# One ring of six PSUM banks for scores and maxima products in an attention stage

## The chip, the cores and the metric

One Trainium2 chip, one of its cores. The metric is the device time of the kernel in microseconds (us). Three runs of the kernel before gave 1196.69, 1202.45 and 1202.41 us, median 1202.41. The execution that was profiled took 1201.56 us, 1199.8 of them between its first and last instruction.

## The reference, cut to what matters

A transformer block in float32: layer norm, cross attention with a residual, layer norm, a mixture of experts with a residual. The change lies in the attention alone:

```
qh, kh, vh = heads of (layernorm(x) @ Wq.T), (ctx @ Wk.T), (ctx @ Wv.T + bv)   # 4 batches, 16 heads of 32
scores = einsum('bhsd,bhtd->bhst', qh, kh) / sqrt(32)        # 1024 x 1024 for each head
scores = where(t >= s, -inf, scores), but (0, 0) stays       # strictly causal
out    = softmax(scores) @ vh                                # then @ Wo.T + bo
```

## The kernel before

After the projections the attention runs in 16 loops (`NIT`), one for each batch and group of four heads (`HG`). A loop needs the queries and keys of its four heads as stacks of 96 rows (high and low parts, so that one product per block is precise enough), in one of three slots (`SLOTS`).

The work is done twice over the same stacks. First come the **maxima**: for each block of 128 queries the product with its keys, in pieces called chunks, 48 a loop (`NC`), 16 early ones for the first 512 queries (`FIRST`, with the diagonal block always at the end of the piece) and 32 late ones (`LATE`). PE writes a chunk to a PSUM bank (line 1151), DVE reduces it to a column of maxima (lines 928 and 931). When the 16 early ones are there, PE turns the columns into rows (the early turn, line 1161), ACT negates them (line 1042), and SP writes the rows by DMA into row 96 of the query stack (line 702, `place_row`). The 32 late ones are followed by a late turn in the same way. Then come the **scores**, transposed (keys on partitions), where the 97th row subtracts the maximum: 12 steps of key blocks by 512 queries, four heads each; PE writes them (line 1172), ACT takes the exponential into `p_t` (line 1064), POOL masks diagonal blocks, and PE multiplies by the values (line 1191) and by ones for the sums (line 1205).

PE's order is written out by hand. A loop has six groups of two steps. In group g, `full_width` (lines 1210 to 1224) issues eight scores of the group that follows, and between them as many chunks **of the next loop** as `SHARE[g]` says (eight numbers, one ahead of each score). Then come the values and sums of group g. The late turn of the loop stands ahead of the third score of group 0; the early turn of the next loop at the head of group `EARLY_AT`, the first group by whose start all 16 early chunks are issued:

```
PER = [sum(share) for share in SHARE]
EARLY_AT = 1 + min(g for g in range(len(GROUPS)) if sum(PER[:g + 1]) >= EARLY)
```

The first chunk of a loop (`c == 0`) is the first product of group 0. It waits for the whole load of its slot, ten DMAs (`chunk`, its wait on `loaded`). Scores cycle through banks 0 to 2 by their own number (`SB + n % SR`) and wait for the exponential three units back; chunks and turns cycle through banks 3 to 5 and wait for the maximum (or the negation) three places back. Bank 6 holds the output, bank 7 the sums. Units of narrow steps hold two or four heads in one bank (`TOGETHER`).

SP's queue is in program order too. In each loop `it` (from line 764 on):

```
place_row(2 * it + 1)                 # late row of this loop
if it > 0: store(it - 1, 1)
if it + 1 < NIT: place_row(2 * it + 2)    # early row of the next loop; waits for m_row_ready
if it + 2 < NIT:
    sp.wait_ge(step_done, it * NS + FETCH)
    load(sp, it + 2)                  # six DMAs of queries, three of keys, one of values
store(it, 0)
```

So the load of loop it + 2 is issued in loop it, for the first chunk of group 0 of loop it + 1. There are 14 such loads.

Of the kernel before, what the change touches and what calls it, by code (L numbers as in the profile page):

```python
# [9 lines left out]
ACT = mybir.ActivationFunctionType  # L10
AX = mybir.AxisListType

P = 128
B, S, D = 4, 1024, 512
H, HD = 16, 32
HG = 4
# [390 lines left out]
def project_attend_route(nc, a, m, keep):  # L407

    NIT = B * NG
    ST = S // P  # L410
    R = 3 * HD
# [4 lines left out]
    NS = len(STEPS)  # L416
    SPAN = [(max(CH * sh, P * j), CH * (sh + 1) - max(CH * sh, P * j)) for sh, j in STEPS]
    TOGETHER = [CH // w if w <= CH // 2 else 1 for _, w in SPAN]
    UNITS = [HG // n for n in TOGETHER]
    UNIT0 = [sum(UNITS[:k]) for k in range(NS + 1)]  # L420
    DIAG = [k for k, (sh, j) in enumerate(STEPS) if P * j >= CH * sh]

    FIRST = [(0, 0), (3, 1), (2, 2), (3, 2), (2, 1), (0, 2), (1, 3), (3, 0), (2, 0), (0, 1), (1, 0), (2, 3), (1, 1),
             (1, 2), (0, 3), (3, 3)]
    LATE = [(2, 5, 0), (1, 4, 1), (2, 7, 0), (0, 7, 0), (3, 5, 1), (3, 6, 1), (0, 5, 0), (3, 6, 0), (2, 7, 1),
# [3 lines left out]
    CHUNKS = [(h, i, 0, (i + 1) * P, True) for h, i in FIRST]  # L429
    EARLY = len(CHUNKS)  # L430
    for h, i, diag in LATE:
        CHUNKS.append((h, i, CH, (i + 1) * P - CH, True) if diag else (h, i, 0, CH, False))
    assert len(set(FIRST)) == HG * ST // 2 and len(set(LATE)) == HG * ST
    NC = len(CHUNKS)
    TRIED = [sum(c[3] for c in CHUNKS[:n] if c[4]) for n in range(NC + 1)]

    GROUPS = [[k, k + 1] for k in range(0, NS, 2)]
# [8 lines left out]
    INVERSIONS = {1: 1, 3: 0}  # L446
    TURN_SLOT = 2

    SHARE = [[1, 2, 0, 1, 1, 2, 1, 0], [0, 2, 0, 2, 1, 2, 1, 1], [4, 0, 1, 1, 1, 1, 0, 2], [1, 0, 0, 1, 0, 2, 2, 1],
             [1, 1, 0, 0, 1, 3, 0, 1], [2, 1, 0, 2, 1, 0, 0, 1]]  # L450

    def portions(g, chunks):
        return SHARE[g] if chunks else [0] * (2 * HG)

    PER = [sum(share) for share in SHARE]
    EARLY_AT = 1 + min(g for g in range(len(GROUPS)) if sum(PER[:g + 1]) >= EARLY)
    TAKES = [PER] * (NIT - 1) + [[0] * len(GROUPS)]
    BEFORE, total = {}, NC
# [8 lines left out]
    TURN_AT = SPOTS[EARLY + 1]  # L467
    AHEAD = [(k, h) for k in GROUPS[0] for h in range(HG)]
    RINGS = {}

    with ExitStack() as ctx:
        def sb(name, shape, dt):
# [5 lines left out]
        def sem(name):  # L478
            return ctx.enter_context(nc.semaphore(name))
# [38 lines left out]
        ks, qs, vt = [k_stack0, k_stack1, k_stack2], [q_stack0, q_stack1, q_stack2], [v_tile0, v_tile1, v_tile2]  # L518
# [28 lines left out]
        t_hi = put("t_hi", [P, KD, CH], F32R, o_at)  # L547
        t_lo = put("t_lo", [P, KD, CH], F32R, sum_at)
        bank = ctx.enter_context(nc.psum_tensor("p2_bank", [P, 8, 512], F32))
        SR, MR = 3, 3  # L550
        SB, MX, OB, DB = 0, 3, 6, 7
        VB, FB, KB = 0, 2, 4

        piece_in = [sem(f"piece_in{k}") for k in range(KD)]
# [45 lines left out]
        exp_done = sem("exp_done")  # L600
# [27 lines left out]

        ring = []
        first_ring = []  # L630

        def place(kind, n):

            RINGS[kind, n] = (MX + len(ring) % MR, ring[-MR] if len(ring) >= MR else None)
            ring.append((kind, n))

        def place_first(kind, n):

            RINGS[kind, n] = (FB + len(first_ring) % 2, first_ring[-2] if len(first_ring) >= 2 else None)
            first_ring.append((kind, n))  # L640

        for spot, n in OURS.items():
            place_first("chunk", n)
            if spot == TURN_AT:
                place_first("turn", 0)
        for it in range(NIT):
            for g in range(len(GROUPS)):
                first = sum(portions(g, TAKES[it][g])[:TURN_SLOT])
                if g == EARLY_AT and it + 1 < NIT:
                    place("turn", 2 * it + 2)  # L650
                for n in range(TAKES[it][g]):
                    if n == first and g == 0:
                        place("turn", 2 * it + 1)
                    place("chunk", BEFORE[it, g] + n)
                if TAKES[it][g] <= first and g == 0:
                    place("turn", 2 * it + 1)

        def fetch_q(eng, it, half, done):

# [24 lines left out]
        with nc.Block() as block:  # L684
# [162 lines left out]
            def _(dve):  # L847
# [62 lines left out]
                def maximum(n):  # L910
# [9 lines left out]
                    col = h * (ST // 2) + i % (ST // 2)  # L920
                    got = bank[:, RINGS["chunk", n][0], 0:w]
                    if diag:
# [104 lines left out]
            def _(act):  # L1027
# [8 lines left out]
                def negate(turn):  # L1036
# [3 lines left out]
                    if it > 0:  # L1040
                        act.wait_ge(m_placed, (turn - 1) * 16)
                    act.activation(m_row[late][:], bank[0:HG * ST // 2, RINGS["turn", turn][0], 0:P], ACT.Copy,
                                   scale=-1.0).then_inc(m_row_ready, 1)
# [9 lines left out]
                def exponential(it, k, u):  # L1053
                    w, m = SPAN[k][1], TOGETHER[k]
                    n = it * UNIT0[NS] + UNIT0[k] + u
                    act.wait_ge(scored, n + 1)
                    if it == 0 and k == 2 and u == 0:
                        act.wait_ge(k_stored, 32 * NCH)
                    if u == 0 and it * NS + k >= SLOTS_P:
                        act.wait_ge(step_done, it * NS + k - SLOTS_P + 1)  # L1060
                        old = (it * NS + k - SLOTS_P) // NS, (k - SLOTS_P) % NS
                        if old[1] in FULL:
                            act.wait_ge(joined, (old[0] * JOINS + max(1, FULL.index(old[1]))) * HG)
                    act.activation(pt[:, k % SLOTS_P, u * m:(u + 1) * m, 0:w],  # L1064
                                   bank[:, SB + n % SR, 0:m * w].rearrange("p (m w) -> p m w", m=m), ACT.Exp,
                                   scale=SCALE).then_inc(exp_done, 1)

                for k in range(KD):
# [62 lines left out]
            def _(pe):  # L1131
                def reuse(kind, n):

                    where, before = RINGS[kind, n]
                    if before is not None and before[0] == "chunk":
                        pe.wait_ge(mx_read, before[1] + 1)
                    if before is not None and before[0] == "turn":
                        pe.wait_ge(m_row_ready, before[1] + 1)
                    return where

                def chunk(n):
# [12 lines left out]
                def turn(t):  # L1154
                    it, late = t // 2, t % 2
                    if late:
                        pe.wait_ge(mx_ready, it + 1)
                    else:
                        pe.wait_ge(mx_read, it * NC + EARLY)
                    to = reuse("turn", t)  # L1160
                    pe.transpose(bank[0:HG * ST // 2, to, 0:P], (mx_l if late else mx_e)[:], ident[:]).then_inc(mx_turned, 1)

                def score(it, k, h):
                    slot, (sh, j), m = it % SLOTS, STEPS[k], TOGETHER[k]
                    n, w = it * UNIT0[NS] + UNIT0[k] + h // m, SPAN[k][1]
                    if it < SLOTS and h == 0 and k == 0:
                        pe.wait_ge(row_ready, it + 1)
                    if h == 0 and k in (0, 4):
                        pe.wait_ge(m_placed, 16 * (2 * it + (1 if k == 0 else 2)))
                    if n >= SR and h % m == 0:  # L1170
                        pe.wait_ge(exp_done, n - SR + 1)
                    mm = pe.matmul(bank[:, SB + n % SR, h % m * w:(h % m + 1) * w], ks[slot][0:R + 1, h, j * P:(j + 1) * P],  # L1172
                                   qs[slot][0:R + 1, sh, h, CH - w:CH], start=True, stop=True)
                    if h % m == m - 1:
                        mm.then_inc(scored, 1)
# [34 lines left out]
                def full_width(it, g):  # L1210

                    if g == EARLY_AT and it + 1 < NIT:
                        turn(2 * it + 2)
                    at, nxt = (it, GROUPS[g + 1]) if g + 1 < len(GROUPS) else (it + 1, GROUPS[0]) if it + 1 < NIT else (it, [])
                    ahead = [(k, h) for k in nxt for h in range(HG)]
                    n = BEFORE[it, g]
                    for i, count in enumerate(portions(g, TAKES[it][g])):
                        if g == 0 and i == TURN_SLOT:
                            turn(2 * it + 1)
                        for _ in range(count):  # L1220
                            chunk(n)
                            n += 1
                        if ahead:
                            score(at, *ahead[i])
# [479 lines left out]
```

## Time and profile before

| | |
|---|---|
| median of three runs | 1202.41 us |
| the profiled execution | 1201.56 us |
| its span | 1199.8 us |
| PE busy | 95% of the span |
| DVE, ACT, POOL busy | 73%, 50%, 45% |
| mean granted TensorE clock | 0.980 |

The profile is of that one execution. Its starts are us from the first instruction. Ends of matmuls are modelled: the engine is busy by these rows where it only waits between starts, so the distance from one start to the next is the better reading. "Idle before" is the idle time of an engine ahead of an instruction, with what ended it. A DMA has two rows: its issue on SP, and the time to its landing.

### The profile page before, as it was taken

The numbers are of one execution on the slowest core, as the hardware profiler recorded it, in microseconds if no ns is written. First come the engines' busy times: TensorE is split into PE (matmuls) and PEld (weight loads), VectorE is DVE, ScalarE is ACT, GpSimd is POOL, SyncE is SP. The second block draws the span as 40 slices with busy tenths as digits, with TensorE's granted clock in tenths as the row PEclk, the third lists the DMA queues.
The fourth block names the chain that finished last, engine by engine and source line by source line (L and its number), as shares of the span: only waits on it lengthen the run. The fifth ranks groups of instructions, "written<-read, shape, count | busy, mean of one in ns | idle before, by whom it ended". The sixth has DMA issues, their size and how long they took to land. (4 is left out here: it accounts for less than half of the span.)

```text
span 1199.8 us, 28725 instructions
## 1 busy us (share of the span) xinstructions
PE 1143.6 (95%) x11328; PEld 785.4 (65%) x11328; DVE 872.1 (73%) x2202; ACT 602.5 (50%) x1108; POOL 535.1 (45%) x738
## 2 busy tenths in 40 slices
PE   7999999999999999999999999998999997778996
PEld 6787888887555555555555555554688877775665
DVE  6755777773777778777787777875598886664866
ACT  4322222223566666566666566667344434446874
POOL 1000000012666668776666777767766630000443
PEclk9999999999899999999999999999999998997998
DMA  8979887967554445666444566621499964845666
GB/s 289 332 259 299 270 320 246 309 205 223 132 125 105 107 106 126 142 141 135 104 108 106 124 133 141 142 75 63 158 312 315 309 239 140 266 144 172 176 176 176
DMA packets 178341, 223.43 MB, mean 186 GB/s; under 512 B 9888, under 2 KB 105632, under 8 KB 177952
## 3 DMA queue, kind: packets, MB, share of 16 engines
q1 hardware_dynamic: 178208, 221.61, 63.2%
q8 instruction: 88, 1.44, 0.5%
q14 instruction: 45, 0.37, 0.1%
HBM read 143.69 MB, written 77.63 MB: 184 GB/s over the span
## 5 line engine op out<-in xcount | busy, mean ns | idle before, releaser
L1064 ACT ACTIVATE p_t<-p_bank 128x512 f32<-128x512 f32 (+1 forms) x608 | 309.6, 577 | 164.6 <-PE p_bank L1172 160.7
L928 DVE CUSTOM_DVE_ANT_0 tried<-p_bank,ban 128x128 bf16<-128x128 f32 (+3 forms) x512 | 231.4, 486 | 108.7 <-PE p_bank L1151 106.3
L1151 PE MATMUL p_bank<-k_stack,q_stack 96*128 96x512 f32 (+3 forms) x768 | 260.7, 380 | 0.4 <-DMA k_stack<-k_hi 0.3
L1172 PE MATMUL p_bank<-q_stack,k_stack 97*128 97x512 f32 (+3 forms) x768 | 234.3, 357 | 4.8 <-ACT p_t L1064 3.2
L1151 PEld LDWEIGHTS p_bank<-k_stack,q_stack 96*128 96x128 f32 x768 | 141.8, 190 | 107.3 <-issue 36.9
L931 DVE TENSOR_REDUCE mx_ab<-p_bank 128x1 f32<-128x512 f32 x256 | 169.3, 686 | 3.3 <-PE p_bank L1151 0.2
L813 POOL TENSOR_SCALAR_AFFINE_SELECT p_t<-p_t 128x128 f32<-128x128 f32 (+2 forms) x288 | 103.2, 361 | 145.5 <-ACT p_t L1064 139.8
L1191 PE MATMUL p_bank<-p_t,v_tile 128*32 128x512 f32 (+3 forms) x1536 | 164.5, 496 | 0.2 <-POOL p_t L809 0.2
L824 POOL TENSOR_TENSOR p_sum<-p_sum,p_t 128x512 f32<-128x512 f32 x128 | 160.4, 1284 | 0.0
L1172 PEld LDWEIGHTS p_bank<-q_stack,k_stack 97*128 97x128 f32 x768 | 137.2, 191 | 26.1 <-ACT p_t L1064 8.3
L1447 POOL TENSOR_TENSOR kept_o_sum<-kept_o_sum,kept_x_in 128x512 f32<-128x512 f32 x30 | 38.4, 1281 | 177.7 <-ACT kept_o_sum L1475 177.0
L795 POOL MEMSET k_stack<- 1x4096 f32 x1 | 3.5, 3517 | 218.1 <-DVE c_lo L996 218.1
L1513 DVE STREAM_TRANSPOSE y_rows<-kept_wide 128x1024 f32<-128x1024 f32 x64 | 73.0, 1209 | 33.3 <-ACT kept_wide L1469 33.3
L1205 PE MATMUL p_bank<-p_t,ones 128*32 128x512 f32 (+3 forms) x1024 | 94.2, 436 | 0.0
L824 POOL TENSOR_TENSOR p_sum<-p_t 128x512 f32<-128x512 f32 x64 | 80.9, 1296 | 5.7 <-ACT p_t L1064 5.7
L1191 PEld LDWEIGHTS p_bank<-p_t,v_tile 128*32 128x32 f32 x1536 | 40.7, 109 | 64.6 <-issue 53.8
L1469 ACT COPY kept_wide<-p_bank 128x1024 f32<-128x1024 f32 x64 | 62.5, 1023 | 14.8 <-PE p_bank L1585 14.0
L1482 ACT COPY kept_wide<-p_bank 128x1024 f32<-128x1024 f32 x32 | 35.1, 1116 | 47.1 <-PE p_bank L1550 46.5
L1205 PEld LDWEIGHTS p_bank<-p_t,ones 128*32 128x32 f32 x1024 | 33.5, 111 | 37.8 <-issue 32.3
L1230 PE MATMUL p_bank<-c_hi,w_hi 128*128 128x512 f32 x128 | 51.5, 402 | 6.1 <-DVE wk_lo L945 6.1
L357 PE MATMUL p_bank<-wo_hi,o_hi 128*128 128x512 f32 x128 | 55.3, 432 | 0.0
L1094 ACT CAST q_hi_s<-p_bank 128x512 fp32r<-128x512 f32 x32 | 18.7, 587 | 68.9 <-PE p_bank L1232 68.9
(133 smaller groups left out, 2108.5 us busy)
## 6 DMA issues: line engine op xcount, KB each, us to landing
q_stack<-q_hi SPq DMA_DIRECT2D x64, 256.0 KB, 6.5
k_stack<-k_hi SPq DMA_DIRECT2D x30, 512.0 KB, 9.8
x_in<-in_x SPq DMA_DIRECT2D x8, 1024.0 KB, 10.1
x_t<-in_x_t SPq DMA_DIRECT2D x8, 1024.0 KB, 9.2
k_hi<-k_hi_s SPq DMA_DIRECT2D x8, 1024.0 KB, 6.2
k_lo<-k_lo_s SPq DMA_DIRECT2D x8, 1024.0 KB, 8.1
v_rows<-v_out SPq DMA_DIRECT2D x8, 1024.0 KB, 7.7
q_hi<-q_hi_s SPq DMA_DIRECT2D x8, 1024.0 KB, 4.3
```

What stands on the lines that cost most here:

```text
L357: pe.matmul(bank[:, A + i % 2], oh, wo_hi[:, k], start=(k == 0), stop=False)
L813: pool.affine_select(part, part, [[0, m], [1, P]], ALU.is_ge, 0.0, base=-1, channel_multiplier=-1).then_inc(masked, 1)
L824: pool.tensor_tensor(p_sum[:, h], first, pt[:, FULL[n] % SLOTS_P, h], ALU.add).then_inc(joined, 1)
L928: dve.tensor_tensor_reduce(scrap, got, ban0[:] if i == 0 else ban[:, CH - w:CH], 1.0, -3e38, ALU.add, ALU.max, to[:, col:col + 1]).then_in ...
L931: dve.tensor_reduce(to[:, col:col + 1], got, AX.X, ALU.max).then_inc(mx_read, 1)
L1064: act.activation(pt[:, k % SLOTS_P, u * m:(u + 1) * m, 0:w], bank[:, SB + n % SR, 0:m * w].rearrange("p (m w) -> p m w", m=m), ACT.Exp, sc ...
L1151: pe.matmul(bank[:, to, 0:w], qs[it % SLOTS][0:R, i * P // CH, h, i * P % CH:i * P % CH + P], ks[it % SLOTS][0:R, h, t0:t0 + w], start=Tru ...
L1172: mm = pe.matmul(bank[:, SB + n % SR, h % m * w:(h % m + 1) * w], ks[slot][0:R + 1, h, j * P:(j + 1) * P], qs[slot][0:R + 1, sh, h, CH - w ...
L1191: mm = pe.matmul(bank[h * HD:(h + 1) * HD, OB, c0:c0 + w], vt[it % SLOTS][:, j, h * HD:(h + 1) * HD], pt[:, k % SLOTS_P, h, 0:w], start=(k ...
L1205: mm = pe.matmul(bank[h * HD:(h + 1) * HD, DB, c0:c0 + w], ones[:], of, start=(k in (0, 4)), stop=(k in (3, NS - 1)), tile_position=(0, h ...
L1469: act.copy(to, bank[:, n % RING * 2:n % RING * 2 + 2].rearrange("p q (m d) -> p d m q", m=2)).then_inc(kept_y, 1)
L1513: ins = dve.transpose(y_rows[ch][:, :, d:d + ONCE].rearrange("p a d b -> p d a b"), y[u % 2][:, ch * P + d:ch * P + d + ONCE])
```

## The change

Scores, chunks and turns share six banks (0 to 5) in one ring, in PE's order; each product waits for whatever stood in its bank before, be it a chunk, a turn or a score. Banks 6 and 7 stay. The first scores of the first loop keep banks 0 to 2. The order of the chunks (`FIRST`, `LATE`) and the numbers between scores (`SHARE`) are replaced. Chunks, scores, values and sums are the same in number and size. The rows of `SHARE` summed (`PER`) were 8, 9, 10, 7, 7, 7 and become 6, 8, 8, 7, 11, 8; `EARLY_AT` follows from them by its unchanged line, as 2 before and 3 after.

```diff
-    FIRST = [(0, 0), (3, 1), (2, 2), (3, 2), (2, 1), (0, 2), (1, 3), (3, 0), ...]
+    FIRST = [(1, 0), (3, 1), (3, 2), (0, 2), (0, 3), (2, 3), (1, 2), (0, 0), ...]
-    LATE = [(2, 5, 0), (1, 4, 1), (2, 7, 0), ...]
+    LATE = [(0, 5, 1), (1, 6, 0), (2, 7, 1), ...]
...
-    SHARE = [[1, 2, 0, 1, 1, 2, 1, 0], [0, 2, 0, 2, 1, 2, 1, 1], [4, 0, 1, 1, 1, 1, 0, 2], [1, 0, 0, 1, 0, 2, 2, 1],
-             [1, 1, 0, 0, 1, 3, 0, 1], [2, 1, 0, 2, 1, 0, 0, 1]]
+    SHARE = [[2, 1, 3, 0, 0, 0, 0, 0], [1, 2, 1, 1, 1, 0, 0, 2], [2, 1, 1, 0, 1, 1, 0, 2], [2, 0, 1, 0, 1, 1, 2, 0],
+             [2, 0, 0, 0, 2, 0, 2, 5], [1, 1, 1, 3, 0, 0, 0, 2]]
...
+    def following(it, g):
+        at, nxt = (it, GROUPS[g + 1]) if g + 1 < len(GROUPS) else (it + 1, GROUPS[0]) if it + 1 < NIT else (it, [])
+        return at, [(k, h) for k in nxt for h in range(HG)]
...
-        SR, MR = 3, 3
-        SB, MX, OB, DB = 0, 3, 6, 7
+        SHARED, AHEAD_BANKS = 6, 3
+        OB, DB = 6, 7
...
-        def place(kind, n):
-            RINGS[kind, n] = (MX + len(ring) % MR, ring[-MR] if len(ring) >= MR else None)
-            ring.append((kind, n))
+        holder = {}
+        def place(kind, n, where):
+            RINGS[kind, n] = (where, holder.get(where))
+            holder[where] = (kind, n)
+        def place_next(kind, n):
+            place(kind, n, len(ring) % SHARED)
+            ring.append((kind, n))
...
+                for i, count in enumerate(portions(g, TAKES[it][g])):
+                    if g == 0 and i == TURN_SLOT:
+                        place_next("turn", 2 * it + 1)
+                    for _ in range(count):
+                        place_next("chunk", n)
+                        n += 1
+                    if ahead and ahead[i][1] % TOGETHER[ahead[i][0]] == 0:
+                        place_next("score", unit_of(at, *ahead[i]))
...
# in reuse():
+                    if before is not None and before[0] == "score":
+                        pe.wait_ge(exp_done, before[1] + 1)
...
# in score():
-                    if n >= SR and h % m == 0:
-                        pe.wait_ge(exp_done, n - SR + 1)
-                    mm = pe.matmul(bank[:, SB + n % SR, ...], ...)
+                    to = reuse("score", n) if h % m == 0 else RINGS["score", n][0]
+                    mm = pe.matmul(bank[:, to, ...], ...)
```

## Rows read from the trace of the kernel before

**Rows 1.** The page, parts 1 and 2: busy time, slices, granted clock.
```profile
PE 1143.6 (95%) x11328; PEld 785.4 (65%) x11328; DVE 872.1 (73%) x2202; ACT 602.5 (50%) x1108; POOL 535.1 (45%) x738
...
PEclk9999999999899999999999999999999998997998
```
**Rows 2.** PE's wait rows of chunks (first three), then of scores (last), by releaser.
```profile
  DVE mx_ab L928: 21.4, 60
  DVE mx_ab L931: 16.9, 60
  DVE mx_e L928: 10.8, 44
...
  ACT p_t L1064: 11.5, 24
```
**Rows 3.** Timeline of PE: first products of groups 0 and 1 of one loop.
```profile
469.61 0.33 PE L1151 MATMUL p_bank<-k_stack,q_stack 96*128 96x128 f32 x1
...
475.10 0.50 PE L1172 MATMUL p_bank<-q_stack,k_stack 97*128 97x512 f32 x1
```
**Rows 4.** Timeline of PE, same loop: group 2, start of 3, next group 0.
```profile
481.34 0.28 PE L1161 MATMUL p_bank<-ident,mx_e 128*16 128x128 f32 x1
...
484.10 0.40 PE L1172 MATMUL p_bank<-q_stack,k_stack 97*128 97x512 f32 x1
484.34 0.40 PE L1151 MATMUL p_bank<-k_stack,q_stack 96*128 96x512 f32 x1
...
488.74 0.44 PE L1151 MATMUL p_bank<-k_stack,q_stack 96*128 96x384 f32 x1
...
504.41 0.33 PE L1151 MATMUL p_bank<-k_stack,q_stack 96*128 96x128 f32 x1
```
**Rows 5.** Timeline of SP in that loop: what its queue issues, and when.
```profile
479.35 0.33 SPq L696 DMA_DIRECT2D o_t<-o_n  x1
481.94 0.52 SPq L702 DMA_DIRECT2D q_stack<-m_row  x1
482.50 1.05 SPq L663 DMA_DIRECT2D q_stack<-q_hi  x2
...
487.35 0.43 SPq L675 DMA_DIRECT2D v_tile<-v_rows  x1
```
**Rows 6.** The values' DMAs (the last of each load), all 16: landing min/median/max.
```profile
DMA to landing us min/median/max: 6.6/14.2/14.9
```
**Rows 7.** Stages: us; PE, PEld, DVE, ACT, POOL busy; clock; DMA share; GB/s.
```profile
484.00:488.00 4.00, 4.00 (x29) 1.78 (x31) 3.87 (x11) 2.71 (x6) 3.33 (x6) 1.00 1.02 243
488.00:492.00 4.00, 4.00 (x23) 2.25 (x15) 3.45 (x10) 2.39 (x5) 4.00 (x5) 1.00 1.03 213
...
500.00:501.00 1.00, 1.00 (x6) 0.81 (x5) 0.86 (x4) 1.00 (x3) 1.00 (x2) 1.00 0.96 314
501.00:502.00 1.00, 1.00 (x8) 0.83 (x6) 1.00 (x2) 1.00 (x3) 1.00 (x2) 1.00 0.01 4
```
**Rows 8.** Timeline of DVE at the end of a loop.
```profile
504.88 0.29 DVE L928 CUSTOM_DVE_ANT_0 tried<-p_bank,ban 128x128 bf16<-128x128 f32 x1 [1.29 <-PE p_bank L1151]
```
**Rows 9.** Stages around low clock, columns as in rows 7.
```profile
1037.00:1039.60 2.60, 0.02 (x3) 0.02 (x4) 1.03 (x1) 0.89 (x1) 0.00 (x0) 1.00 0.07 20
1039.90:1043.30 3.40, 3.40 (x70) 3.40 (x66) 1.34 (x2) 1.25 (x2) 0.00 (x0) 0.50 1.08 291
...
299.00:306.00 7.00, 7.00 (x27) 4.29 (x29) 4.48 (x17) 4.39 (x8) 1.17 (x4) 0.51 0.00 0
...
834.00:838.50 4.50, 2.86 (x16) 1.21 (x8) 3.94 (x3) 2.42 (x6) 4.50 (x5) 1.00 0.00 0
838.50:842.00 3.50, 3.50 (x25) 0.99 (x24) 0.00 (x0) 1.07 (x3) 3.50 (x4) 0.51 0.20 75
```
**Rows 10.** Stage of the attention's steady loops, columns as in rows 7.
```profile
342.00:818.00 476.00, 475.87 (x3634) 266.44 (x3630) 374.97 (x1183) 296.88 (x601) 350.56 (x549) 1.00 0.53 120
```
**Rows 11.** Timeline of PE in the first loop: groups 1, 2, 3, next loop's start.
```profile
298.30 0.50 PE L1172 MATMUL p_bank<-q_stack,k_stack 97*128 97x512 f32 x1 [1.61 <-DMA q_stack<-m_row]
...
307.35 0.28 PE L1161 MATMUL p_bank<-ident,mx_e 128*16 128x128 f32 x1
...
314.74 0.44 PE L1151 MATMUL p_bank<-k_stack,q_stack 96*128 96x384 f32 x1
...
330.41 0.33 PE L1151 MATMUL p_bank<-k_stack,q_stack 96*128 96x128 f32 x1
```

More of the change, by code:

```diff
@@ L421, in project_attend_route @@
     DIAG = [k for k, (sh, j) in enumerate(STEPS) if P * j >= CH * sh]
-    FIRST = [(0, 0), (3, 1), (2, 2), (3, 2), (2, 1), (0, 2), (1, 3), (3, 0), (2, 0), (0, 1), (1, 0), (2, 3), (1, 1),
-             (1, 2), (0, 3), (3, 3)]
-    LATE = [(2, 5, 0), (1, 4, 1), (2, 7, 0), (0, 7, 0), (3, 5, 1), (3, 6, 1), (0, 5, 0), (3, 6, 0), (2, 7, 1),
[3 rows of a table removed]
+    FIRST = [(1, 0), (3, 1), (3, 2), (0, 2), (0, 3), (2, 3), (1, 2), (0, 0), (3, 0), (3, 3), (0, 1), (2, 2), (1, 3),
+             (1, 1), (2, 0), (2, 1)]
+    LATE = [(0, 5, 1), (1, 6, 0), (2, 7, 1), (1, 7, 0), (3, 4, 0), (2, 5, 0), (0, 4, 1), (1, 6, 1), (3, 5, 1),
[3 rows of a table added]
     CHUNKS = [(h, i, 0, (i + 1) * P, True) for h, i in FIRST]
@@ L630, in project_attend_route, with unit_of @@
         first_ring = []
-        def place(kind, n):
-            RINGS[kind, n] = (MX + len(ring) % MR, ring[-MR] if len(ring) >= MR else None)
+        holder = {}
[4 more added lines that the diff above has]
+            place(kind, n, len(ring) % SHARED)
             ring.append((kind, n))
+        def unit_of(it, k, h):
+            return it * UNIT0[NS] + UNIT0[k] + h // TOGETHER[k]
         def place_first(kind, n):
@@ L645, in project_attend_route @@
                 place_first("turn", 0)
+        for n, (k, h) in enumerate(AHEAD):
+            if h % TOGETHER[k] == 0:
+                place("score", unit_of(0, k, h), unit_of(0, k, h) % AHEAD_BANKS)
         for it in range(NIT):
             for g in range(len(GROUPS)):
-                first = sum(portions(g, TAKES[it][g])[:TURN_SLOT])
+                at, ahead = following(it, g)
                 if g == EARLY_AT and it + 1 < NIT:
[L650 to L656, printed above, removed]
+                    place_next("turn", 2 * it + 2)
+                n = BEFORE[it, g]
+                for i, count in enumerate(portions(g, TAKES[it][g])):
[6 more added lines that the diff above has]
+                        place_next("score", unit_of(at, *ahead[i]))
         def fetch_q(eng, it, half, done):
@@ L1064, in exponential @@
                     act.activation(pt[:, k % SLOTS_P, u * m:(u + 1) * m, 0:w],
-                                   bank[:, SB + n % SR, 0:m * w].rearrange("p (m w) -> p m w", m=m), ACT.Exp,
+                                   bank[:, RINGS["score", n][0], 0:m * w].rearrange("p (m w) -> p m w", m=m), ACT.Exp,
                                    scale=SCALE).then_inc(exp_done, 1)
@@ L1169, in score @@
                         pe.wait_ge(m_placed, 16 * (2 * it + (1 if k == 0 else 2)))
-                    if n >= SR and h % m == 0:
-                        pe.wait_ge(exp_done, n - SR + 1)
-                    mm = pe.matmul(bank[:, SB + n % SR, h % m * w:(h % m + 1) * w], ks[slot][0:R + 1, h, j * P:(j + 1) * P],
+                    to = reuse("score", n) if h % m == 0 else RINGS["score", n][0]
+                    mm = pe.matmul(bank[:, to, h % m * w:(h % m + 1) * w], ks[slot][0:R + 1, h, j * P:(j + 1) * P],
                                    qs[slot][0:R + 1, sh, h, CH - w:CH], start=True, stop=True)
@@ L1213, in full_width @@
                         turn(2 * it + 2)
-                    at, nxt = (it, GROUPS[g + 1]) if g + 1 < len(GROUPS) else (it + 1, GROUPS[0]) if it + 1 < NIT else (it, [])
-                    ahead = [(k, h) for k in nxt for h in range(HG)]
+                    at, ahead = following(it, g)
                     n = BEFORE[it, g]
```

6 rows, old and new, of the table LATE are left out of this document.

## The prediction

> **What bounds the kernel now.** First the page's totals: PE is busy for 95% of the span, DVE for 73%, at a granted clock that is 2.4 GHz (10 tenths) nearly throughout [rows 1]. PE is the bound. Modelled ends hide its waits, so I go by starts. From 342 to 818 us the attention runs at clock 1.00 [rows 10]. One of its loops starts at 469.61 and the next at 504.41 [rows 3, 4]: 34.80 us a loop. Two 512-wide products follow each other in 0.24 us where nothing is waited for (484.10, 484.34) [rows 4].
>
> Second, what the ring is about: how long PE's queue waited for a bank. For chunks 21.4 + 16.9 + 10.8 = 49.1 us over the kernel, for scores 11.5 [rows 2]. These 60.6 us are all that a better use of the six banks could win; the other waits are not for banks.
>
> Third, SP's queue and the DMAs, because the change moves the early turn. In the loop shown the early turn is on PE at 481.34 [rows 4], SP sends the row at 481.94, and only behind it the next load, from 482.50 to the values' DMA at 487.35 [rows 5], which lands a median 14.2 us later, 14.9 at most [rows 6]. The DMA engines are full meanwhile (share 1.02 and 1.03) and idle from 501 on (0.01) [rows 7]. The first chunk that needs this load starts at 504.41 [rows 4]. So this load ends some 3 us before it is waited for, and costs nothing: the chain early turn, row, load, next loop is nearly as long as what PE does beside it.
>
> **The change part by part.**
>
> *The early turn, and the load behind it.* The new numbers sum to 6, 8, 8 in the first three groups in place of 8, 9, 10. After two groups 17 chunks were issued, and now 14; so the early turn goes from the head of group 2 to that of group 3. In SP's queue that moves the early row, all ten DMAs of the load behind it, and the store of the first half behind those. The wait on the landing stays with the first product of group 0, and PE is in order: all of the next loop stands behind it.
>
> From the turn to the last issue it is 487.35 - 481.34 = 6.0 us [rows 4, 5], and to the landing 14.2 more [rows 6]: 20.2 us. What PE has to do between the head of group 3 and the next group 0 was 504.41 - 488.74 = 15.7 us [rows 4]. Chunks of groups 3 to 5 grow from 16.75 widths of 512 to 20.5 (counted from `FIRST`, `LATE`, `SHARE`): 3.75 x 0.235 = 0.9 us more, 16.6 us. The load is then late by 20.2 - 16.6 = 3.6 us, in each loop.
>
> The new period is the time from the loop's start to the new turn, and 20.2. The first term was 488.74 - 469.61 = 19.1 us [rows 3, 4]. It loses the same 3.75 widths, 0.9 us. Of its bank waits I let 0.5 us go, nearly all of it because after a wait for the load group 0 finds all banks read out and ACT and DVE idle (DVE's last idle time there is 1.29 us even now [rows 8]). 19.1 - 0.9 - 0.5 + 20.2 = 37.9, which is 3.1 more than 34.8. Fourteen loads: 44 us. In the first loop the head of group 3 is at 314.74 and the next loop at 330.41 [rows 11], the same 15.7 us apart, so it pays the same.
>
> Bounds. Without any bank wait groups 0 to 2 take less: chunks' and scores' waits are 60.6 / 16 = 3.8 us a loop [rows 2], and 2.1 of it for these three groups, which hold 39 of the loop's 72 widths of 512; the period is then 19.1 - 0.9 - 2.1 + 20.2 = 36.3, +1.5 a loop, +21 us. Should the new order instead wait a microsecond more in these groups, and each load land at the 14.9 of the slowest, the period is 19.1 - 0.9 + 1.0 + 6.0 + 14.9 = 40.1, +5.3 a loop, +74 us. Inside these bounds I take 44.
>
> *The ring.* The instructions are the same, one wait ahead of each product as before. A score may now stand behind a chunk's maximum and a chunk behind an exponential; the run of six scores at the end of group 0 may go six banks deep. By rows 2 it is worth between +60.6 us (if waits double) and -60.6. But groups 3 to 5 now end before the load does: what they win or lose, up to 3.6 us, vanishes in the wait for it. Only groups 0 to 2 count, and there I have given 0.5. The last two loops wait for no load; I take nothing for them, 1.5 us each way at most by the 3.8 a loop.
>
> *Widths.* Same chunks, other order. Chunks in the projections sit in a ring of two banks that stays. I take nothing: PE's wait for `mx_e` is 10.8 us in all [rows 2], a few of them there. The late turn has three chunks ahead of it both times. The early row is needed by group 5: it is issued 0.6 us after the turn [rows 4, 5], two groups ahead. Nothing late here.
>
> *The clock.* PE will stand still for 3.6 us and a little in each loop. What the trace shows of such gaps: PE does 0.02 us of work in 1037.0 to 1039.6 and is at 0.50 (1.2 GHz) from 1039.9 to 1043.3; it is busy for 2.86 of the 4.5 us up to 838.5, and at 0.51 for 3.5 us; the first loop, whose group 1 waited 1.61 us for a row [rows 11], is at 0.51 from 299 to 306 [rows 9]. In this last place the price can be read: from the start of group 1 to the early turn 307.35 - 298.30 = 9.05 us [rows 11] against 481.34 - 475.10 = 6.24 [rows 3, 4], 2.8 us for 7 us of low clock, 0.4 a microsecond. A gap of 3.6 us is longer than all that fell before, so I expect a low stretch of 3.4 us in most of the 14 loops: 1.4 us, less what lies still in the gap, 1.3. 14 x 1.3 = 18 us. Bounds: nothing, and 2.8 in each, 39 us.
>
> The Trainium skill has the same thing in "TensorE: Matmul & The Clock Gate", section "HAM oscillation — how this bites in real kernels": a loop that waits for its DMA in every turn starts every turn at half clock. Rows 9 agree for single gaps; a repeated one is in no row of the kernel before. By that rule the 18 us are certain, and without it the time is the one of the first rival. The same page, "A second HAM failure mode: psum-queue depth-cycling", says that short pauses of PE from cycling through PSUM banks make the clock swing as well. That speaks for the clock being at stake in the ring itself, but the trace disagrees: with 3.8 us of bank waits a loop, spread out, the clock is 1.00 over 476 us [rows 2, 10].
>
> **Sum.** Against its own execution: 1201.56 + 44 + 18 = 1264 us. The median of before is 0.8 us above that execution, which changes nothing.
>
> **Rivals.**
>
> (1) *The load is late, the clock holds.* 1201.6 + 44 = 1246. For it: a low stretch follows idle time only in stages where PE has less to do otherwise, and the gap here ends in dense work. Against: the three falls in rows 9. The late load alone may also be anywhere in +21 to +74.
>
> (2) *The banks decide, the load does not.* The other side. Were the load landed by the end of group 5, PE's bank waits are the term: half of 60.6 won gives 1171. It happens if the ten DMAs move faster than before: in its last microsecond the load ran at 314 GB/s against 213 to 243 in the middle [rows 7]; at 314 throughout the 14.2 us shrink by about a quarter, 20.2 - 3.6 = 16.6, exactly what PE needs. That is the point from which it decides. Against: the DMA engines are at share 1.0 in both stretches, the ten DMAs are the same, and nothing that slows them (the store, PE's stream) leaves.
>
> (3) *The turn moves, but something keeps the load early.* The load waits in SP's queue for the row and nothing else; unless my count of `EARLY_AT` is wrong this cannot be. Then the time is that of the ring alone, 1195 to 1210.
>
> **How the numbers follow.** Load late with the clock falling in most loops: 0.68, 1264, own range 1245 to 1285. Late, clock holding: 0.26, 1246, from 1219. Rival 2: 0.03. Rival 3: 0.03. The predicted time is 1264. The range takes 1236 to 1284: below it lie the rivals 2 and 3 and the lower part of rival 1, above it both upper bounds together (1201.6 + 74 + 39 = 1315). A change under 0.5% (6 us) cannot be told from none here. Faster by more than that: 0.03; within: 0.02; slower: 0.95.
>
> **What would show it.** The early turns of the steady loops 38 to 39 us apart, each at the head of group 3. SP's load issued some 1.2 us behind it, landing 20 us behind it. Ahead of the first chunk of each loop from the second to the fifteenth PE idle for 3 to 5 us, put down to a DMA of the load. A granted clock of 0.5 for a few us right behind many of these gaps, none of it in the last two loops; the mean clock falls from 0.98 to about 0.96. PE's waits for ACT or DVE in groups 3 to 5 may be anything. Wrong, if the gap is not there, or if it is and the loop is still 34.8 us; half wrong, if the clock stays at 1.00.

## The result, and the profile after

The changed kernel takes 1252.68 us in the median of four runs (1249.36 to 1261.87), the one before 1202.43: a ratio of 1.043, 95% interval 1.039 to 1.046, slower. The forecast was 1264 (1236 to 1284). The profiled execution took 1249.44 us, with a span of 1247.7, 47.9 more than before.

The page of the changed kernel, its totals and slices, beside rows 1:

```profile
PE 1135.4 (91%) x11328; PEld 803.1 (64%) x11328; DVE 865.1 (69%) x2202; ACT 601.4 (48%) x1108; POOL 534.2 (43%) x738
...
PEclk9999999999899998999989989999999999997999
```

PE fell from 95% to 91%. Its busy time fell by only 8 us (1143.6 to 1135.4), while its idle time doubled, from 56 us of the span to 112. The groups of instructions say where (us busy, mean ns of one, idle before with its releaser):

```profile
L1172 PE MATMUL p_bank<-k_stack,q_stack 96*128 96x512 f32 (+3 forms) x768 | 243.8, 379 | 52.3 <-DMA v_tile<-v_rows 51.0
```

The releaser is the values' DMA, the last of a load. The waits of PE (us in all, times, longest) say that it is 14 times, as many as there are loads:

```profile
PE p_bank L1172 <- DMA v_tile<-v_rows: 51.0, 14, 4.5
```

One loop of the changed kernel, in PE's timeline. In each row the first number is the start; line 1172 holds the chunks, 1182 the turns:

```profile
444.08 0.50 PE L1172 MATMUL p_bank<-k_stack,q_stack 96*128 96x128 f32 x2 [3.25 <-DMA v_tile<-v_rows]
...
462.25 0.28 PE L1182 MATMUL p_bank<-ident,mx_e 128*16 128x128 f32 x1
...
483.25 0.80 PE L1172 MATMUL p_bank<-k_stack,q_stack 96*128 96x128 f32 x2 [4.51 <-DMA v_tile<-v_rows]
...
502.43 0.28 PE L1182 MATMUL p_bank<-ident,mx_e 128*16 128x128 f32 x1
```

Start to turn 18.2 us, turn to next start 21.0, the last 4.5 of them idle; then 19.2 to the next turn. Before, a loop was 34.80 us without a gap [rows 3, 4]. SP's timeline after that turn:

```profile
462.86 0.51 SPq L721 DMA_DIRECT2D q_stack<-m_row  x1
463.42 1.25 SPq L682 DMA_DIRECT2D q_stack<-q_hi  x2
...
469.02 0.46 SPq L694 DMA_DIRECT2D v_tile<-v_rows  x1
469.53 4.33 SPq L715 DMA_DIRECT2D o_t<-o_n  x1
```

The row, then the load, 0.6 and 1.2 us behind the turn, as before it was [rows 5], but one group later. The landing is unchanged (before: [rows 6]):

```profile
DMA to landing us min/median/max: 6.5/14.0/14.7
```

The clock in the gap and behind it, for two loops (columns as in rows 7):

```profile
440.80:444.00 3.20, 0.03 (x4) 0.00 (x0) 0.00 (x0) 0.59 (x1) 0.19 (x1) 1.00 1.10 259
444.50:448.00 3.50, 3.50 (x14) 3.11 (x12) 3.16 (x13) 1.92 (x6) 0.82 (x3) 0.51 0.03 6
448.00:480.00 32.00, 30.75 (x253) 17.56 (x252) 23.98 (x75) 19.74 (x40) 24.56 (x38) 1.00 0.52 115
482.20:488.90 6.70, 5.64 (x23) 4.36 (x27) 4.39 (x15) 2.98 (x7) 1.80 (x6) 0.50 0.02 4
```

In the gap PE works for 0.03 of 3.2 us while the DMA engines are full (1.10). Then it runs at 1.2 GHz for 3.5 us, in the other loop for 6.7, of which the first 1.1 still lie in the gap. All 14 gaps are followed by such a stretch; before, there was none from 342 to 818 us [rows 10].

The thirteen loops that wait for a load and are waited for in turn lie between these two starts:

```profile
329.51 0.80 PE L1172 MATMUL p_bank<-k_stack,q_stack 96*128 96x128 f32 x2 [4.08 <-DMA v_tile<-v_rows]
...
833.18 0.50 PE L1172 MATMUL p_bank<-k_stack,q_stack 96*128 96x128 f32 x2 [3.20 <-DMA v_tile<-v_rows]
```

503.67 / 13 = 38.74 us a loop, 3.94 more than 34.80: 51.2 us, slightly more than the whole loss. In these thirteen loops the low stretch behind the start is the short one eight times and the long one five times.

### The profile page after: what moved, and what is told of

It reads as the page before. It is cut to its first block and busy times, and to the rows that moved or that the text cites. A ratio compares the mean times of both kernels' runs of the same rounds, so it can differ in the third digit from the quotient of the medians.

```text
span 1247.7 us, 28724 instructions
## 1 busy us (share of the span) xinstructions
PE 1135.4 (91%) x11328; PEld 803.1 (64%) x11328; DVE 865.1 (69%) x2202; ACT 601.4 (48%) x1108; POOL 534.2 (43%) x738
## 3 DMA queue, kind: packets, MB, share of 16 engines
q1 hardware_dynamic: 178208, 221.61, 60.6%
## 5 line engine op out<-in xcount | busy, mean ns | idle before, releaser
L1083 ACT ACTIVATE p_t<-p_bank 128x512 f32<-128x512 f32 (+1 forms) x608 | 304.7, 590 | 199.4 <-PE p_bank L1192 194.8
L947 DVE CUSTOM_DVE_ANT_0 tried<-p_bank,ban 128x512 bf16<-128x512 f32 (+3 forms) x512 | 231.0, 487 | 168.5 <-PE p_bank L1172 167.9
L1172 PE MATMUL p_bank<-k_stack,q_stack 96*128 96x512 f32 (+3 forms) x768 | 243.8, 379 | 52.3 <-DMA v_tile<-v_rows 51.0
L1192 PE MATMUL p_bank<-q_stack,k_stack 97*128 97x512 f32 (+3 forms) x768 | 229.9, 372 | 1.8 <-DMA q_stack<-m_row 1.3
L1211 PE MATMUL p_bank<-p_t,v_tile 128*32 128x512 f32 (+3 forms) x1536 | 167.6, 505 | 4.4 <-POOL p_t L832 3.9
L1192 PEld LDWEIGHTS p_bank<-q_stack,k_stack 97*128 97x128 f32 x768 | 146.7, 207 | 30.9 <-ACT p_t L1083 7.9
L950 DVE TENSOR_REDUCE mx_ab<-p_bank 128x1 f32<-128x512 f32 x256 | 163.7, 683 | 0.0
L843 POOL TENSOR_TENSOR p_sum<-p_sum,p_t 128x512 f32<-128x512 f32 x128 | 160.3, 1284 | 0.0
L1488 ACT COPY kept_wide<-p_bank 128x1024 f32<-128x1024 f32 x64 | 62.4, 1020 | 19.2 <-PE p_bank L1604 18.7
L1249 PE MATMUL p_bank<-t_hi,w_hi 128*128 128x512 f32 x128 | 50.9, 397 | 1.4 <-issue 1.4
```

Source lines behind the costliest of these rows:

```text
L843: pool.tensor_tensor(p_sum[:, h], first, pt[:, FULL[n] % SLOTS_P, h], ALU.add).then_inc(joined, 1)
L947: dve.tensor_tensor_reduce(scrap, got, ban0[:] if i == 0 else ban[:, CH - w:CH], 1.0, -3e38, ALU.add, ALU.max, to[:, col:col + 1]).then_in ...
L950: dve.tensor_reduce(to[:, col:col + 1], got, AX.X, ALU.max).then_inc(mx_read, 1)
L1083: act.activation(pt[:, k % SLOTS_P, u * m:(u + 1) * m, 0:w], bank[:, RINGS["score", n][0], 0:m * w].rearrange("p (m w) -> p m w", m=m), AC ...
L1172: pe.matmul(bank[:, to, 0:w], qs[it % SLOTS][0:R, i * P // CH, h, i * P % CH:i * P % CH + P], ks[it % SLOTS][0:R, h, t0:t0 + w], start=Tru ...
L1192: mm = pe.matmul(bank[:, to, h % m * w:(h % m + 1) * w], ks[slot][0:R + 1, h, j * P:(j + 1) * P], qs[slot][0:R + 1, sh, h, CH - w:CH], sta ...
```

## The experiments

Theory: the sums of `SHARE` move the early turn a group later, SP issues the load behind it, the load ends after PE needs it, and the gap lowers the clock. Rival: the shared ring, or the new orders, make PE wait for banks. Eight kernels in two sets of four; the kernel before ran beside each set, at 1203.31 and 1201.77 us.

**The turn alone, in the old kernel.**

```diff
-    EARLY_AT = 1 + min(g for g in range(len(GROUPS)) if sum(PER[:g + 1]) >= EARLY)
+    EARLY_AT = 3
```

> The kernel before with one line changed: the early turn stands at the head of group 3 instead of group 2; three-bank rings, chunks and numbers between scores as before. Theory (the moved turn makes each load late, and the gap lowers the clock): the loop start to the turn takes 19.1 us here against 18.2 in the changed kernel, and the load another 20.3, so the period is 39 to 40 us, 14 loops at +4 to +5: 1260 to 1270 us, slower than the changed kernel itself, with PE idle 3 to 5 us ahead of 14 loops. Rival (the ring or the new order costs the time): 1202 us, no gap.

1304.33 us, ratio 1.085 (1.081 to 1.088), above the 1260 to 1270 expected. The mechanism alone, without ring or orders, does it and does it worse. PE's timeline of this kernel:

```profile
414.29 0.47 PE L1151 MATMUL p_bank<-k_stack,q_stack 96*128 96x128 f32 x1 [3.84 <-DMA v_tile<-v_rows]
...
435.70 0.28 PE L1161 MATMUL p_bank<-ident,mx_e 128*16 128x128 f32 x1
...
456.58 0.47 PE L1151 MATMUL p_bank<-k_stack,q_stack 96*128 96x128 f32 x1 [5.13 <-DMA v_tile<-v_rows]
```

21.4 + 20.9 = 42.3 us, where I expected 39 to 40. Over thirteen loops the two parts are 21.7 and 20.2 us in the mean. The second is as expected; in the first I had left out the low clock, which followed all 14 gaps, for 6.8 or 10.2 us each time: 19.1 became 21.7. The size was wrong for that reason, not the direction.

**The ring alone, with the old orders and numbers.** The changed kernel with `FIRST`, `LATE` and `SHARE` of before.

> The changed kernel with the old orders of chunks and the old numbers between scores: only the shared ring is new, the early turn is back at the head of group 2. Theory: no gap ahead of a loop, clock 1.00 in the steady loops, and only the ring's own effect, at most 60 us of bank waits won and likelier between 1185 and 1215. Rival (the ring is what costs): over 1230 us with PE's waits for ACT and DVE up from 60 us.

1196.98 us, ratio 0.994 (0.992 to 0.997). Two starts of loops in PE's timeline, 34.61 us apart and with no idle time ahead:

```profile
433.99 0.33 PE L1172 MATMUL p_bank<-k_stack,q_stack 96*128 96x128 f32 x1
...
468.60 0.33 PE L1172 MATMUL p_bank<-k_stack,q_stack 96*128 96x128 f32 x1
```

The ring costs nothing and wins 0.2 us a loop. That is 3 of the 6 us; the rest lies outside the steady loops, where it can't be told from the spread described in the last section. The rival falls for the ring.

**Two chunks earlier.** The changed kernel, with the turn back at group 2 by its own rule:

```diff
-    SHARE = [..., [1, 2, 1, 1, 1, 0, 0, 2], ..., [2, 0, 0, 0, 2, 0, 2, 5], ...]
+    SHARE = [..., [1, 2, 1, 1, 1, 1, 1, 2], ..., [2, 0, 0, 0, 2, 0, 2, 3], ...]
```

> The changed kernel with two chunks moved from group 4 to group 1 (sums 6, 10, 8, 7, 9, 8), so that 16 chunks stand ahead of group 2 and the early turn goes back there. Ring and orders as changed. Theory: the load is in time again, the period falls from 37.7 to 39.7 us to 33.5 to 35, and the whole is 1175 to 1205 us. Rival (the new numbers and widths cost the time by bank waits): 1235 us or more, periods over 37 us without a gap.

1193.96 us, ratio 0.992 (0.989 to 0.995). PE's timeline, two starts 34.44 us apart and without a gap:

```profile
431.13 0.50 PE L1172 MATMUL p_bank<-k_stack,q_stack 96*128 96x128 f32 x2
...
465.57 0.50 PE L1172 MATMUL p_bank<-k_stack,q_stack 96*128 96x128 f32 x2
```

Ring, new orders and nearly all new numbers are in it, and it is slightly faster than before. Two of 48 chunks in another place are worth 59 us.

**The gap filled.** The changed kernel with 14 products more ahead of the wait for the load; they compute nothing that is used:

```diff
                     elif c == 0:
+                        if 2 <= it:
+                            for _ in range(14):
+                                pe.matmul(bank[:, reuse("chunk", n), 0:512], qs[(it - 1) % SLOTS][0:R, 0, 0, 0:P], ks[(it - 1) % SLOTS][0:R, 0, 0:512],
+                                          start=True, stop=True)
                         pe.wait_ge(loaded[it % SLOTS], ...)
```

> The changed kernel with 14 products more (old data, 512 wide, 3.3 us at full clock) ahead of the wait for the load, into the bank that the first chunk then overwrites: PE is busy in most of the gap, everything else is the same. Theory (the low clock behind the gap lengthens the way to the turn): clock 1.00 at the loop starts, loop start to turn at most 18.2 us in all loops against 18.2 to 19.7, about 10 us less in 14 loops, 1235 to 1243 us. Rival (the low clock costs nothing, only the load counts): 1249 to 1254 us. If the extra products come too late into the gap and hold PE up: above 1255 us.

1240.49 us (1235.96 to 1243.08), 12 us less than the changed kernel, with more work. PE's timeline (the start of loop 1, then a loop in the middle) and a stage of the steady loops:

```profile
330.05 0.50 PE L1176 MATMUL p_bank<-k_stack,q_stack 96*128 96x128 f32 x2 [0.66 <-DMA v_tile<-v_rows]
...
437.54 3.47 PE L1172 MATMUL p_bank<-k_stack,q_stack 96*128 96x512 f32 x14
441.42 0.50 PE L1176 MATMUL p_bank<-k_stack,q_stack 96*128 96x128 f32 x2 [0.41 <-DMA v_tile<-v_rows]
...
458.18 0.28 PE L1186 MATMUL p_bank<-ident,mx_e 128*16 128x128 f32 x1
```
```profile
326.00:844.00 518.00, 512.15 (x3920) 311.57 (x3920) 377.98 (x1218) 302.46 (x616) 355.11 (x561) 1.00 0.49 113
```

The clock is 1.00 in all loops. From the first true chunk to the turn it is 458.18 - 441.42 = 16.8 us, against 18.2 and 19.2 above: the price of the low clock by itself, 1.4 us for the short stretch and 2.4 for the long one (of which 5.6 us lie behind the start). From the start of loop 1 to that of the last loop it is 844.3 - 330.1 = 514 us, against 867.8 - 329.5 = 538 in the changed kernel. That is 24 us less; the code behind took 14 more in the profiled execution (394.0 us against 379.9, last section), so that 9 are left there, and 12 in the medians. By the rule of the Trainium skill, "TensorE: Matmul & The Clock Gate", "HAM oscillation — how this bites in real kernels", a loop's own DMA wait is what throttles it anew each turn. These two kernels agree, with 14 low stretches in 14 gaps and none where the gap is filled; with shorter gaps it was not each turn (orders alone, below).

**One wait split.** The changed kernel, whole, but with the load's last four DMAs (second half of the queries, values) on a semaphore of their own, for which the first late chunk waits, in place of the first chunk:

```diff
-            fetch_q(eng, it, 1, done)
-            fetch_v(eng, it)
+            fetch_q(eng, it, 1, late_in[it % SLOTS])
+            fetch_v(eng, it, late_in[it % SLOTS])
...
-                        pe.wait_ge(loaded[it % SLOTS], LOADS * (it // SLOTS + (it % SLOTS > 0)) + 16 * (it % SLOTS == 0))
+                        pe.wait_ge(loaded[it % SLOTS], 96 * (it // SLOTS + (it % SLOTS == 2)) + (16, 160, 0)[it % SLOTS])
+                    elif c == EARLY and it >= 2:
+                        pe.wait_ge(late_in[it % SLOTS], 64 * (it // SLOTS + (it % SLOTS == 2)))
```

> The changed kernel, whole, with one wait split: the first chunk of a loop waits only for the six DMAs that it and the early chunks need (first half of the queries, keys), the sixteenth late one (the first late chunk) for the other four. Turn, queue order, ring, orders as changed. Theory (the wait for the load is the whole loss, and it drew the clock down): six DMAs land about 14 us after the turn, PE needs 16.4; no gap, clock 1.00, period 16.8 + 16.4 = 33.2 to 33.8 us, 15 loops at -1.0 to -1.6: 1178 to 1190 us. Rival (some other part of the new order costs time that the gap now hides): period 34.5 us or more, 1200 us or more.

1180.68 us (1178.85 to 1182.82), ratio 0.982 (0.980 to 0.984): faster than both kernels, with the turn where the change put it. PE's timeline:

```profile
463.88 0.50 PE L1175 MATMUL p_bank<-k_stack,q_stack 96*128 96x128 f32 x2
...
480.85 0.28 PE L1185 MATMUL p_bank<-ident,mx_e 128*16 128x128 f32 x1
...
497.28 0.50 PE L1175 MATMUL p_bank<-k_stack,q_stack 96*128 96x128 f32 x2
```

17.0 + 16.4 = 33.4 us, clock 1.00. Of the load for the first start shown (463.88), the six DMAs had landed at 461.94, 1.9 us ahead of it, and the values landed at 468.35, 4.5 us behind it. So ring, orders and numbers are good for 1.4 us a loop, and what the changed kernel lost, 72 us in all (1252.7 to 1180.7), hung on one wait that asked for more than it needed.

**The same with three and three banks.** New orders and numbers and the split wait, on the two old rings.

> As the one with the split wait, but with the two old rings of three banks: new orders and new numbers between scores without the shared ring. If the shared ring is what the new numbers need, the runs of six scores wait for exponentials three back: period 1 to 2 us longer than with the shared ring, 1195 to 1215 us. If the orders alone bring the gain: within 5 us of the kernel with the split wait.

1229.28 us, ratio 1.023 (1.022 to 1.025); more than the 1215 I gave as the upper end. Starts of two loops, 36.63 us apart, 3.2 to 3.4 more than with the shared ring:

```profile
437.80 0.50 PE L1154 MATMUL p_bank<-k_stack,q_stack 96*128 96x128 f32 x2
...
474.43 0.50 PE L1154 MATMUL p_bank<-k_stack,q_stack 96*128 96x128 f32 x2
```

What PE's queue waited for here ahead of chunks (first three) and scores (last), the same rows as rows 2:

```profile
  DVE mx_ab L932: 26.0, 75
  DVE mx_ab L929: 14.1, 55
  DVE mx_e L929: 11.2, 44
...
  ACT p_t L1065: 35.3, 114
```

And in the kernel with the shared ring, ahead of chunks (first two) and scores:

```profile
  DVE mx_ab L951: 15.6, 30
  ACT p_t L1084: 6.9, 24
...
  ACT p_t L1084: 8.3, 25
  DVE mx_e L948: 4.1, 23
  DVE mx_ab L951: 3.1, 15
```

With a last row of 0.8 that is 86.6 us of bank waits against 38.8: 48 us, and the times differ by 49. The new numbers need the shared ring, and with the old numbers the ring is worth 6 at most. Neither gives the gain without the other. The same sum of rows was 60.6 us before [rows 2], and it is 57.7 with the ring alone and 51.1 with two chunks earlier, so in the kernels without a late load the time follows the bank waits.

**Orders alone, load late.** The old kernel with the new orders and numbers.

> The kernel before with the new orders and new numbers, rings of three banks as before, the wait for the load whole: the load is late as in the changed kernel. Theory (only groups 0 to 2 and the load make the period): loop start to turn longer by what three banks cost in groups 0 to 2 (up to 1.5 us), turn to next start 20 us as before: 1250 to 1275 us, with the same gaps and low clocks. Rival (the ring made the load late): 1210 us or less.

1272.11 us, ratio 1.061 (1.054 to 1.068): within the range expected, and 19 us more than with the shared ring. With the load late the ring still counts in groups 0 to 2, which stand ahead of the turn. PE's timeline, and the clock in the first loop shown and in the one that follows it:

```profile
445.74 0.50 PE L1151 MATMUL p_bank<-k_stack,q_stack 96*128 96x128 f32 x2 [1.48 <-DMA v_tile<-v_rows]
...
465.40 0.28 PE L1161 MATMUL p_bank<-ident,mx_e 128*16 128x128 f32 x1
...
485.17 0.50 PE L1151 MATMUL p_bank<-k_stack,q_stack 96*128 96x128 f32 x2 [1.54 <-DMA v_tile<-v_rows]
```
```profile
448.00:451.40 3.40, 3.40 (x15) 1.81 (x17) 2.82 (x7) 1.96 (x4) 1.40 (x4) 0.51 0.01 2
485.20:503.60 18.40, 18.20 (x136) 9.93 (x137) 13.80 (x46) 11.60 (x25) 8.88 (x18) 1.00 0.05 16
```

The turn comes 19.7 us after the start (18.2 with the ring, where the low stretch was as short as here), the next loop 19.8 after the turn. The gap is shorter because groups 3 to 5 wait for banks in the same time: from the turn to the next start they take 18.2 us with three banks and no late load (the kernel above), and 16.4 with the shared ring. One thing I had not expected: the gaps here are 1.3 to 2.3 us, and a low clock followed only seven of the 14. Where none did, start to turn is 18.4 to 18.5 us. That took back part of what the missing ring cost; in the profiled executions a loop is 39.3 us in the mean against 38.7 in the changed kernel.

**The load ahead of the row.** The changed kernel with two statements of SP's loop exchanged, so that `load(sp, it + 2)` precedes `place_row(2 * it + 2)`.

> The changed kernel with SP's queue turned around: the load ahead of the early row. The load is then issued at the end of group 1 and in time by far; the row's DMA is issued behind it at the head of group 3 and shares the DMA engines with it. Theory: no gap at the loop's start; if the row lands in its 1.8 us in spite of the load, 1178 to 1190 us; if it has to queue behind the load's packets it lands up to 13 us after the turn, 2 to 3 us too late for group 5, a new gap there with low clock: 1220 to 1250 us. I hold the second for likelier, 6 in 10.

1226.02 us, ratio 1.021 (1.019 to 1.024), the likelier of my two cases. The gap has moved to the first score of group 5 (PE waits there for the row 13 times, 20.9 us in all, and in six of these loops the clock falls behind it), and SP shows why:

```profile
452.49 0.43 SPq L694 DMA_DIRECT2D v_tile<-v_rows  x1
454.31 5.00 SPq L721 DMA_DIRECT2D q_stack<-m_row  x1
```
```profile
466.63 0.50 PE L1192 MATMUL p_bank<-q_stack,k_stack 97*128 97x512 f32 x1 [1.65 <-DMA q_stack<-m_row]
```

The early row of 8 KB takes 5.0 us to issue, where it took 0.52 [rows 5]. The fourteen rows that stand behind a load land 11.5 to 12.8 us after the start of their issue, the late rows 1.8. With the turn at group 3, then, one of the two comes late in either order, as long as the first chunk waits for all ten DMAs; the late row costs less (1226 against 1253 us). What the exchange would do with the turn at group 2 was not run.

## Why the prediction was right

Direction, place and mechanism held: the turn at group 3, SP's order, a gap of 3.0 to 4.5 us ahead of loops 1 to 14 put down to a DMA of the load, a low clock behind each. Four of the eight kernels test these by themselves: the turn moved alone brings the loss to the old kernel, two chunks or a split wait take it from the new one, the filled gap takes only the clock's part.

The terms, by size:

- *Turn to landing*, 20.2 us forecast. The mean from the turn to the next start, 0.04 us behind the landing, is 20.1 over the thirteen loops.
- *PE's work from turn to next start*, 16.6 forecast: 16.4 (497.28 - 480.85). That this fits is luck. With three banks the new numbers make it 18.2 us, by bank waits that I had not counted, and the shared ring takes them away again.
- *Start to turn at full clock*, 17.7 forecast: 16.8 in the kernel with the gap filled. I had let 0.5 us of bank waits go; 1.5 went. This is the mis-sized term, and the reason that I gave for it was wrong too: I put the 0.5 down to the idle time ahead of group 0, in which the banks are read out. With three banks the stretch is 18.4 to 18.5 us whether there is a gap ahead of it (orders alone, loops at full clock) or not (three and three banks). With the shared ring it is 16.7 to 16.8 in the kernel with the gap filled, where the other engines still pause for the load, and 16.9 in the mean with the split wait, where nothing pauses. So the idle time gives 0.1 us at most, and the shared ring some 1.6.
- *Period without the clock*: 16.8 + 20.1 - 34.8 = 2.1 us, times 13 = 27 us, where I had 3.1 x 14 = 44. The fourteenth gap lies at the end of the first loop, where before the change there was a low stretch of 7 us [rows 9] that is not there now; so that loop did not grow (41.5 us, before 41.4). The forecast had it pay like the others.
- *The clock*, 1.3 us a loop and 18 us forecast. Mean start to turn is 18.65 us in the thirteen loops, 1.85 above 16.8: 24 us. The price of 0.4 us for a microsecond at low clock held (1.4 for 3.4, 2.4 for 5.6). What was off is the length: I priced each gap with the short stretch of 3.4 us, and five of thirteen had the long one.

27 + 24 = 51; the attention's other loops and what stands before and behind it give back 3, and 48 are measured. The forecast of 62 was 14 too high: 17 too much for the late load, for the ring more than for anything else, and 3 for what was given back, less 6 too little for the clock. That the errors have opposite signs is luck, and the number is closer for it than its terms.

Of the rivals, the first (clock holding) is what the filled gap shows as a kernel of its own, at 1240 us where I had 1246. The second and third are refuted: the loads land as late as before, and the turn moved. The bank waits of before (60.6 us) turned out to hold a real gain, since the split wait wins 21 us over the kernel before with 22 us less of them.

What stays open: why the low clock lasts 3.4 us behind one gap and 6.8 behind the next of nearly the same length, and why it follows each gap of 3.0 us and more but only half of the gaps of 1.3 to 2.3 us. No run here separates the causes.

## What to carry to other kernels

When numbers in a hand-written order are retuned, follow what is derived from them: here a turn whose place is computed from the sums, and behind it, in another engine's queue, ten transfers. Ask of each load by how much it was early (3 us in 35 here), and whether the first consumer waits for all of it or only for its part: a split wait was worth 72 us for three more semaphores. And a gap that comes in each loop costs more than its length where it lowers PE's clock; by the terms above that was nearly half of the loss.

## What the runs showed of the hardware

A DMA issued right behind the ten of a load costs the issuing engine too: SP needed 4.3 us for the store in the changed kernel and 5.0 us for the row in the one with the load first, against 0.33 and 0.52 us with nothing ahead of them [rows 5]. Over all loops it was 4.3 to 6.7 us for the store and 3.6 to 5.6 us for the row.

From the start of the last loop on, the changed kernel and the two shown here run the same code, and yet it takes a different time from one to the next, with the share of it at low clock. The stage to the end, in the kernel with the gap filled, in the one with the load ahead of the row, and in the changed one (columns as in rows 7):

```profile
844.30:1238.30 394.00, 340.45 (x6133) 267.40 (x6129) 266.48 (x527) 193.75 (x336) 142.86 (x124) 0.93 0.64 201
```
```profile
836.90:1216.20 379.30, 327.63 (x6132) 256.83 (x6129) 265.40 (x527) 194.04 (x336) 142.66 (x124) 0.97 0.66 209
```
```profile
867.80:1247.70 379.90, 329.34 (x6133) 258.33 (x6129) 262.73 (x527) 194.40 (x336) 142.64 (x124) 0.97 0.66 209
```

394.0 us at 0.93 against 379.3 and 379.9 at 0.97. This is of the size of the spread within one kernel's runs (1249.36 to 1261.87 with clocks from 0.964 to 0.953), and of what a small effect on the attention would have to be told apart from. The loops' periods in the trace are free of it.
